# Two more regions for the rows: units five and six read while the loop drains

## The chip, the cores and the metric

The kernel runs on one core of a Trainium2 chip. The metric is the device time of one execution in microseconds (us). A profiled execution also has a span, which is the stretch from its first to its last instruction as the hardware profiler saw it; all positions below ("at 1138 us") are counted from the span's start.

## The reference

Two layers over x of 2 x 4096 tokens by D = 1024 channels, 8192 rows in all.

```python
# layer 1: gated linear recurrence, state S of 64 x 1024 for each sequence
shift = silu(causal_depthwise_conv(x, conv_w, conv_b))          # width 4
r, k  = split(shift @ in_proj_w.T)                               # 64 each
u     = sigmoid(x @ w0.T @ w1.T + b1) * x
sel, tau = softplus(mg[:64]), sigmoid(mg[64:])                   # mg = shift @ mem_gate_w.T + b
k     = k / norm(k) * sel ** tau;   g = -sel * tau
S     = exp(g) * S + k u;           o = r S / 8                  # step by step
y     = layernorm(x + o + shift * residual_weight)
# layer 2: every row chooses one of 64 tiles of 16 channels, by signs
xn    = layernorm(y) * gamma + beta
tile  = best of 64, from sign(xn) against the tiles' signatures
mn, mx = min and max, over ALL rows that chose the tile, of their 16 channels
delta = spline(tile, (xn[16 channels] - mn) / (mx - mn)) * output_scale[tile]
out   = layernorm(y + y + delta put into those 16 channels)
```

The smallest and largest value of a tile go over all rows, so the second half of layer 2 can only begin when layer 1 is done with its last row.

## The kernel before

The kernel consists of two programs in one launch, each written engine by engine with hand-placed semaphores. A barrier over all engines stands between them.

**The first program, the loop.** The rows are worked in 32 groups of 256 (`NG`, `T`), two chunks of 128 rows each. Group k passes through stages that are up to four steps apart, so a step works on several groups at once; SyncE (SP) issues the plain DMAs. For each group SP stores y (the rows before normalisation) twice: to `y_ring`, a small buffer in DRAM, and to `y_scratch`, which holds all rows. Later GpSimd (POOL) issues four indirect DMAs for the group, the gather (L1448 and L1451, `gsl` and `gbs`): for each row the 16 channels of its chosen tile from `y_ring`, and that tile's gamma and beta from a table. It then waits for them at L1465 and computes with them (`collect`, L1465 to L1473, whose last result is `xfs`). VectorE (DVE) takes the extremes over all rows in four parts (`extremes`, L1020 to L1033); the last part, rows of chunks 56 to 63, waits for the collect of the last group. After it comes the barrier. The choice of tile for a group comes from a matmul that TensorE (PE) ends with L474; its event is `e_key`, and e_key of the last group is the last read of the tiles `sg` and `yn`.

**The second program.** The rows come back from `y_scratch` in 16 units of 512 rows (2048 KB each). Units 0 to 14 go round eight places in SBUF (`slots`), unit 15 is still in `y_all`. A unit is read into its place, ScalarE (ACT) scales and shifts it there in four instructions (L1700), and ACT issues its store to `out` (L1707). Beside that PE and DVE work out the spline (`Z`, L1668 to L1823) in seven batches of chunks, POOL turns a batch's sums into coefficients (L1610 to L1619), and POOL puts the 16 corrected channels of each row into `out` by indirect DMAs, the scatters (L1629), one for each chunk of 128 rows, 64 in all; 28 of them come after the last batch's coefficients. A scatter of a unit waits until the unit's store has landed.

**The places.** A place is either a region that the loop's tiles have lain in, over which a unit may be read as soon as the loop has finished with it, or memory of the second program's own. `PRE` counts the former and `OWN` the latter. Before, they are five and three: units 0 and 1 are issued at L410 and L411 when the last group's projections are done, unit 2 at L437 and units 3 and 4 at L440 and L441 after the last state update. Units 5, 6 and 7 have places of their own and are issued at L1578, the first thing that SP does behind the barrier. Units 8 to 14 follow at the same line, each behind a wait for the store of the unit that had its place.

Of the kernel before, what the change touches and what calls it, by code (L numbers as in the profile page):

```python
# [7 lines left out]
F32 = mybir.dt.float32  # L8
BF16 = mybir.dt.bfloat16
F16 = mybir.dt.float16  # L10
# [4 lines left out]
P = 128  # L15
CH = 128
CPG = 2
T = CH * CPG
LEVELS = 7
# [28 lines left out]
def build(nc, x, w_rk, w_mg, w0, w1, conv_w, conv_b, gate_b1, mem_b, res_w, gamma, beta, bases, slopes, oscale, out):  # L48
    B, L, D = x.shape
# [3 lines left out]
    NB = D // P  # L53
    NG = B * L // T
# [5 lines left out]
    TPC = NT // NCL  # L60
    HALF = 512
    TC = 2 * DS * GRID
    PRE, OWN = 5, 3
    EXT_ENDS = (16, 40, 56, 64)
    SLOTS4 = PRE + OWN + 1
    assert TC == HALF
# [14 lines left out]
    with ExitStack() as whole:  # L81
        def sbw(name, shape, dt=F32):
            return whole.enter_context(nc.sbuf_tensor(name, shape, dt))
# [21 lines left out]
        zT_all = sbw("zT_all", [P, 2, NB, T])  # L105
# [13 lines left out]
        with ExitStack() as loop_only:  # L119
# [2 lines left out]
            w0_sb = loop_only.enter_context(nc.sbuf_tensor("w0_sb", [P, NB, R], F32))  # L122
            w1_sb = loop_only.enter_context(nc.sbuf_tensor("w1_sb", [P, D], F32))
        ohT = sbw("ohT", [P, NC, P], BF16)
        slots = [xT_all[:].rearrange("p i b t -> p (i b t)")[:, 0:4 * D].rearrange("p (n d) -> p n d", n=4), rows1[:],
                 rows2[:, 0:4 * D].rearrange("p (n d) -> p n d", n=4), th_all[:],
                 zT_all[:].rearrange("p i b t -> p (i b t)").rearrange("p (n d) -> p n d", n=4)]
        r_ld = [whole.enter_context(nc.semaphore(f"r_ld{i}")) for i in range(SLOTS4)]
        x1s = sbw("x1s", [P, NC, DS])
        xfs = sbw("xfs", [P, NC, DS])  # L130
# [1 line left out]
        with ExitStack() as ctx:  # L132
            def sb(name, shape, dt=F32):
                return ctx.enter_context(nc.sbuf_tensor(name, shape, dt))
# [7 lines left out]
            def ev(name, per_group=1):  # L142
                return Event(sem(name), per_group)
# [33 lines left out]
            xin = [xin_all[:, i, :, :] for i in range(2)]  # L177
            xT = [xT_all[:, i, :, :] for i in range(2)]
            zT = [zT_all[:, i, :, :] for i in range(2)]
            tS = [sb(f"tS{i}", [P, T]) for i in range(2)]  # L180

            rr = sb("rr", [P, CH])
            kk = sb("kk", [P, CH])
            ksq = sb("ksq", [P, CH])
            xs = sb("xs", [P, 2, CH])
            xa = sb("xa", [P, 2, CH])
            ge = sb("ge", [P, 2, CH])
            gl = sb("gl", [P, 2, CH])
            gw1 = sb("gw1", [P, 2, CH])
            grw = sb("grw", [P, 2, CH])  # L190
            sel = sb("sel", [P, CH])
            lsel = sb("lsel", [P, CH])
            tau = sb("tau", [P, CH])
            gn = sb("gn", [P, CH])
            tl = sb("tl", [P, CH])
            nl = sb("nl", [P, CH])
            kn = sb("kn", [P, CH])
            bb = sb("bb", [P, CH])
            rkp = sb("rkp", [P, CH])
            RX = sb("RX", [P, CPG, CH + 1])  # L200
            keT_sb = sb("keT_sb", [P, P])
            Wm = sb("Wm", [P, CPG, LEVELS, CH // 2])
            AT = sb("AT", [P, CPG, CH])
            th = [[th_all[:, CPG * i + c, :] for c in range(CPG)] for i in range(2)]
            S = [sb(f"S{i}", [P, HALF]) for i in range(2)]
            y = [y_all[:, i, :, :] for i in range(2)]
            yn = [sb(f"yn{i}", [P, D]) for i in range(CPG)]
            sg = sb("sg", [P, NB, T], F16)
            key_u = sb("key_u", [P, CPG], U32)
            key_n = sb("key_n", [P, CPG], U32)  # L210
            gix = [sb(f"gix{i}", [P, 2, CPG], U32) for i in range(2)]
# [7 lines left out]
            mm = sb("mm", [P, 2, NC])  # L219
            ext_n = sb("ext_n", [P, 2, NT])  # L220
            scratch = xin_all[:].rearrange("p i c d -> p (i c d)")
            sq = sb("sq", [P, CPG, D], BF16)
            ysum = sb("ysum", [P, CPG])
            nm = [sb(f"nm{i}", [P, CPG]) for i in range(2)]
            ssm = sb("ssm", [P, CPG])
# [58 lines left out]
            e_key, e_km = ev("e_key"), ev("e_km")  # L284
            e_cq, e_ch, e_go, e_cp = ev("e_cq", 2), ev("e_ch"), ev("e_go"), ev("e_cp", 6)

            def wait(eng, e, k, i=0):
                eng.wait_ge(e.sem, e.at(k, i))

            def done(eng, e, k):  # L290

                wait(eng, e, k, e.count - 1)
# [58 lines left out]
            y_u = y_dram.rearrange("(u n p) d -> u p n d", n=4, p=P)  # L351

            @block.sync
            def _(sp):
# [84 lines left out]
                done(sp, e_su[1], NG - 1)  # L439
                sp.dma_start(slots[3], y_u[3]).then_inc(r_ld[3], 16)  # L440
                sp.dma_start(slots[4], y_u[4]).then_inc(r_ld[4], 16)  # L441
                for b in range(2):
                    sp.wait_ge(d_yst[b], NG * 16)

# [1436 lines left out]
```

## Time and profile before

| | |
|---|---|
| time before, median of 3 runs | 1308.65 us (1307.91 to 1309.11) |
| the profiled execution, its own time | 1311.31 us |
| its span | 1309.2 us |
| busy: PE, DVE, ACT, POOL | 1158.9, 1061.5, 951.7, 833.4 us |
| barrier between the programs | at about 1138 us |

The loop takes seven eighths of the span. A row of a timeline gives the start and the duration in us, the engine, the line, the operation, what it writes and reads, how many like it were merged, and in brackets the idle time in front of it and what ended that. A queue's name ends in q (SPq, ACTq): its rows are the issue of a DMA, not its transfer. Names of tiles have their numbers left out, so `own` stands for all three of the second program's own places and `rows` for rows1 and rows2.

### The profile page before, as it was taken

What the parts mean: (1) busy time and instruction counts of PE and PEld (TensorE: products, weight loads), DVE (VectorE), ACT (ScalarE), POOL (GpSimd) and SP (SyncE); (2) the same over time, 40 slices, a digit from 0 to 9 for tenths busy, and PEclk for the clock granted to TensorE, in tenths of its full rate; (3) what the DMA queues carried; (4) which work ended last, traced back from release to release, by engine and by line L of the source; (5) the groups of instructions that cost most, each with busy time, mean ns of one, the idle gap of its engine ahead of it and who ended that gap; (6) DMA issues with size and microseconds to landing.
All of it is one profiled execution on the core that took longest, in us unless ns stands there. A gap on an engine that the chain in (4) does not pass through costs nothing. (4 is left out here: it accounts for less than half of the span.)

```text
span 1309.2 us, 31773 instructions
## 1 busy us (share of the span) xinstructions
PE 1158.9 (89%) x9346; PEld 735.1 (56%) x9346; DVE 1061.5 (81%) x2508; ACT 951.7 (73%) x1809; POOL 833.4 (64%) x1692
## 2 busy tenths in 40 slices
PE   5799999999999999999999999999999965588700
PEld 4556666666666666666666666666666632333100
DVE  4888889999999999999999999998988765586710
ACT  5657888888888888888888888888888743444760
POOL 3125666767676767676767676767676665335576
PEclk9989999999999999999999999999999977655555
DMA  4112222222222222222222222222222116689993
GB/s 141 34 37 102 103 103 104 102 102 102 102 102 102 102 103 106 106 106 106 106 106 106 106 106 106 106 106 106 106 105 102 71 65 234 230 316 352 419 409 125
DMA packets 64115, 175.05 MB, mean 134 GB/s; under 512 B 11580, under 2 KB 23108, under 8 KB 64071
## 3 DMA queue, kind: packets, MB, share of 16 engines
q1 hardware_dynamic: 49430, 138.85, 28.7%
q10 hardware_dynamic: 8496, 33.56, 6.6%
q0 software_dynamic: 6144, 2.11, 1.2%
q8 instruction: 22, 0.36, 0.1%
q14 instruction: 23, 0.18, 0.0%
HBM read 69.06 MB, written 101.20 MB: 130 GB/s over the span
## 5 line engine op out<-in xcount | busy, mean ns | idle before, releaser
L1052 DVE SCALAR_TENSOR_TENSOR acc<-xT_all,cw_sb,acc 128x256 f32<-128x256 f32 x768 | 354.3, 520 | 7.2 <-ACT acc L751 7.1
L777 ACT ACTIVATE sg<-TX,bet,gam 128x256 f16<-128x256 f32 x256 | 129.5, 556 | 42.2 <-PE TX L464 42.2
L484 PE MATMUL PR<-xT_all,w_sb 128*128 128x256 f32 x512 | 139.1, 396 | 2.9 <-ACT xT_all L715 2.9
L1384 POOL TENSOR_TENSOR AT<-AT,Wm 128x128 f32<-128x128 f32 x224 | 114.8, 512 | 41.7 <-DVE AT L1078 25.9
L496 PE MATMUL WK<-w_sb,tS 128*128 128x512 f32 x256 | 138.3, 622 | 0.0
L751 ACT ACTIVATE acc<-xT_all,cb_sb,cw_sb 128x256 f32<-128x256 f32 x256 | 132.5, 592 | 4.8 <-DVE xT_all L1038 2.8
L538 PE MATMUL OB<-th_all,AT 128*128 128x512 f32 x256 | 124.4, 609 | 11.7 <-POOL AT L1384 10.2
L566 PE MATMUL PR<-shT,w_mg_sb 128*64 128x128 f32 x2048 | 128.0, 278 | 6.5 <-ACT shT L760 6.5
L566 PE MATMUL PR<-shT,w_rk_sb 128*64 128x128 f32 x2048 | 125.9, 276 | 0.0
L566 PEld LDWEIGHTS PR<-shT,w_rk_sb 128*64 128x64 f32 x2048 | 110.5, 137 | 26.3 <-issue 26.3
L566 PEld LDWEIGHTS PR<-shT,w_mg_sb 128*64 128x64 f32 x2048 | 112.5, 138 | 18.9 <-issue 12.0
L1396 POOL TENSOR_TENSOR X<-bb 128x64 f32<-128x64 f32 x224 | 91.3, 413 | 48.4 <-DVE bb L1145 45.0
L484 PEld LDWEIGHTS PR<-xT_all,w_sb 128*128 128x128 f32 x512 | 90.0, 195 | 36.8 <-issue 25.1
L1060 DVE SCALAR_TENSOR_TENSOR zT_all<-shT,rw_sb,xT_all 128x256 f32<-128x256 f32 x256 | 106.8, 480 | 1.9 <-PE OB L543 1.5
L1066 DVE SCALAR_TENSOR_TENSOR th_all<-th_all,xin_all 128x1024 f32<-128x1024 f32 x64 | 78.3, 1223 | 33.3 <-ACT th_all L730 33.3
L715 ACT ACTIVATE xT_all<-TX 128x512 f32<-128x512 f32 x128 | 75.5, 590 | 38.9 <-PE TX L455 37.5
L455 PE MATMUL TX<-ident,xin_all 128*128 128x128 f32 x512 | 82.6, 285 | 12.7 <-DMA xin_all<-in_x 7.3
L705 ACT ACT_TABLE_LOAD x72 | 92.4, 1283 | 1.3
L1448 POOL DMA_INDIRECT gsl<-y_ring,gix x64 | 68.6, 1072 | 38.8 <-POOL st L1423 28.9
L464 PE MATMUL TX<-ident,yn 128*128 128x128 f32 x512 | 82.0, 284 | 10.8 <-DVE yn L1212 6.6
L1436 POOL TENSOR_TENSOR nm<-ysum,consts 128x1 f32<-128x1 f32 x64 | 22.3, 348 | 102.9 <-ACT y_all L741 102.9
L455 PEld LDWEIGHTS TX<-ident,xin_all 128*128 128x128 f32 x512 | 59.3, 144 | 48.1 <-issue 29.0
(230 smaller groups left out, 2665.1 us busy)
## 6 DMA issues: line engine op xcount, KB each, us to landing
xin_all<-in_x SPq DMA_DIRECT2D x32, 1024.0 KB
y_ring<-y_all SPq DMA_DIRECT2D x32, 1024.0 KB, 4.1
y_scratch<-y_all SPq DMA_DIRECT2D x32, 1024.0 KB, 6.1
own<-y_scratch SPq DMA_DIRECT2D x5, 2048.0 KB, 16.1
out<-own ACTq DMA_DIRECT2D x5, 2048.0 KB, 19.9
rows<-y_scratch SPq DMA_DIRECT2D x4, 2048.0 KB, 12.3
out<-rows ACTq DMA_DIRECT2D x4, 2048.0 KB, 13.6
RX<-RE SPq DMA_DIRECT2D x128, 32.2 KB
```

What stands on the lines that cost most here:

```text
L455: i = pe.transpose(TX[:, (blk % 2) * T + c * P:(blk % 2) * T + (c + 1) * P], xin[b][:, c, blk * P:(blk + 1) * P], ident[:])
L484: i = pe.matmul(PR[:, 0:T], w0_sb[:, blk, :], xT[b][:, blk, HIST:HIST + T], start=(blk == 0), stop=(blk == NB - 1))
L496: pe.matmul(WK[h][:], tS[b][:, chunk_cols(c)], w1_sb[:, half_cols(h)], start=True, stop=False)
L538: pe.matmul(OB[:, half_cols(h)], AT[:, c, :], th[b][c][:, half_cols(h)], start=True, stop=False)
L566: i = pe.matmul(PR[chunk_rows(c), (at + n) * CH:(at + n + 1) * CH], w[:, blk, n * M:(n + 1) * M], shT[:, blk, chunk_cols(c)], start=(opens ...
L705: nc.scalar.add_instruction(mybir.InstLoadActFuncSet(name=nc.get_next_instruction_name(), act_func_set_id=which))
L751: nc.scalar.activation(acc[:, blk, :], xT[b][:, blk, 0:T], ACT.Identity, scale=cw_sb[:, blk, 0:1], bias=cb_sb[:, blk:blk + 1]).then_inc(e_ ...
L777: nc.scalar.activation(sg[:, blk, :], TX[:, (blk % 2) * T:(blk % 2 + 1) * T], ACT.Sign, scale=gam[:, blk:blk + 1], bias=bet[:, blk:blk + 1 ...
L1052: v.scalar_tensor_tensor(acc[:, blk, :], xT[b][:, blk, i:i + T], cw_sb[:, blk, i:i + 1], acc[:, blk, :], ALU.mult, ALU.add).then_inc(e_con ...
L1060: v.scalar_tensor_tensor(zT[b][:, blk, :], shT[:, blk, :], rw_sb[:, blk:blk + 1], xT[b][:, blk, HIST:HIST + T], ALU.mult, ALU.add).then_in ...
L1384: q.tensor_tensor(late, late, Wm[:, :, l, :].rearrange("p c (n h) -> p c n h", h=h), ALU.add)\
L1396: q.tensor_tensor(x_late, b_late, ref, ALU.subtract)
```

## The change

The small tiles of the gates and the convolution's sums (tS to rkp, and Wm) are laid out together, and a region rows3 is laid over them; the normalised rows, their signs and their squares (yn, sg, sq) are laid out together, and a region rows4 is laid over those. Units 5 and 6 are read into these two. The number of places stays at eight.

```diff
-    PRE, OWN = 5, 3
+    PRE, OWN = 7, 1
...
+            tS = [lsb(f"tS{i}", [P, T]) for i in range(2)]
+            rr = lsb("rr", [P, CH])
...
+            rkp = lsb("rkp", [P, CH])
+            Wm = lsb("Wm", [P, CPG, LEVELS, CH // 2])
+        rows3 = sbw("rows3", [P, 7 * T + 14 * CH + LEVELS * CH])
...
+            yn = [lsb(f"yn{i}", [P, D]) for i in range(CPG)]
+            sg = lsb("sg", [P, NB, T], F16)
+            sq = lsb("sq", [P, CPG, D], BF16)
+        rows4 = sbw("rows4", [P, 4, D])
...
-                 zT_all[:].rearrange("p i b t -> p (i b t)").rearrange("p (n d) -> p n d", n=4)]
+                 zT_all[:].rearrange("p i b t -> p (i b t)").rearrange("p (n d) -> p n d", n=4),
+                 rows3[:, 0:4 * D].rearrange("p (n d) -> p n d", n=4), rows4[:]]
...
                 sp.dma_start(slots[4], y_u[4]).then_inc(r_ld[4], 16)
+                sp.dma_start(slots[5], y_u[5]).then_inc(r_ld[5], 16)
+                done(sp, e_key, NG - 1)
+                sp.dma_start(slots[6], y_u[6]).then_inc(r_ld[6], 16)
                 for b in range(2):
                     sp.wait_ge(d_yst[b], NG * 16)
```

The first place is SP's list at the end of the first program, from the last group's stores to the barrier, before the change; in brackets is what an instruction waits for, and rows is rows2.

```order
L363 DMA y_ring<-y_all 128x2x1024 [waits e_y]
L364 DMA y_scratch<-y_all 128x2x1024
L437 DMA rows<-y_scratch 128x4x1024 [waits e_dec,d_rx,e_keT,e_A]
L440 DMA th_all<-y_scratch 128x4x1024 [waits e_su,e_o]
L441 DMA zT_all<-y_scratch 128x4x1024
L132 UNCONDITIONAL_BRANCH [waits d_yst1,d_yst0]
L1575 UNCONDITIONAL_BRANCH [waits barrier_Pool_Activation_PE_DVE_SP_release]
```

The same place after the change; rows is rows2, then rows3 and rows4.

```order
L374 DMA y_ring<-y_all 128x2x1024 [waits e_y]
L375 DMA y_scratch<-y_all 128x2x1024
L448 DMA rows<-y_scratch 128x4x1024 [waits e_dec,d_rx,e_keT,e_A]
L451 DMA th_all<-y_scratch 128x4x1024 [waits e_su,e_o]
L452 DMA zT_all<-y_scratch 128x4x1024
L453 DMA rows<-y_scratch 128x4x1024
L455 DMA rows<-y_scratch 128x4x1024 [waits e_key]
L166 UNCONDITIONAL_BRANCH [waits d_yst1,d_yst0]
L1589 UNCONDITIONAL_BRANCH [waits barrier_Pool_Activation_PE_DVE_SP_release]
```

Unit 5 is now issued directly behind unit 4 and waits for nothing more; unit 6 follows behind a wait for e_key of the last group.

The second place is SP's list at the start of the second program, before the change; p_st is the store of the unit that had the place.

```order
L1578 DMA own<-y_scratch 128x4x1024 x3
L1578 DMA xT_all<-y_scratch 128x4x1024 [waits p_st0]
L1578 DMA rows<-y_scratch 128x4x1024 [waits p_st1]
L1578 DMA rows<-y_scratch 128x4x1024 [waits p_st2]
L1578 DMA th_all<-y_scratch 128x4x1024 [waits p_st3]
L1578 DMA zT_all<-y_scratch 128x4x1024 [waits p_st4]
L1578 DMA own<-y_scratch 128x4x1024 [waits p_st5]
```

The same after the change.

```order
L1592 DMA own<-y_scratch 128x4x1024
L1592 DMA xT_all<-y_scratch 128x4x1024 [waits p_st0]
L1592 DMA rows<-y_scratch 128x4x1024 [waits p_st1]
L1592 DMA rows<-y_scratch 128x4x1024 [waits p_st2]
L1592 DMA th_all<-y_scratch 128x4x1024 [waits p_st3]
L1592 DMA zT_all<-y_scratch 128x4x1024 [waits p_st4]
L1592 DMA rows<-y_scratch 128x4x1024 [waits p_st5]
```

Only unit 7 is left of the three reads behind the barrier; all later reads wait for the same stores.

The third place is POOL's list at the end of the first program after the change, the last group's gather and its collect; apart from line numbers it reads the same before it.

```order
L1462 DMA gsl<-y_ring,gix 128x16 [waits e_cp,e_ch,d_yst1]
L1465 DMA gbs<-gb_table,gix 128x32
L1462 DMA gsl<-y_ring,gix 128x16
L1465 DMA gbs<-gb_table,gix 128x32
L1479 COPY last_all<-gix 128x2 [waits e_keep,d_gat1]
L1480 TENSOR_TENSOR xc<-gsl,nm_all 128x32
```

Nothing moves here, nor on PE and DVE; on ACT only the places of units 5, 6, 13 and 14 have other names.

## Rows read from the trace of the kernel before

**Rows 1.** The page: the span, and its DMA share in 40 slices.

```profile
span 1309.2 us, 31773 instructions
...
DMA  4112222222222222222222222222222116689993
```

**Rows 2.** Timeline of POOL in the second program: a wait for sums, and the last scatters.

```profile
1228.18 0.23 POOL L1610 TENSOR_SCALAR mean_n<-sums 128x12 f32<-128x12 f32 x1 [11.68 <-DVE sums L1823]
...
1267.20 1.07 POOL L1629 DMA_INDIRECT out<-outs,gidx  x1 [0.86 <-DVE outs L1808]
...
1301.39 0.96 POOL L1629 DMA_INDIRECT out<-outs,gidx  x1 [0.30 <-issue]
```

**Rows 3.** Timeline of ACT in the second program: units 5 and 6.

```profile
1200.95 4.63 ACT L1700 ACTIVATE own<-own,coef 128x1024 f32<-128x1024 f32 x4 [0.46 <-ACT zT_all L1700]
...
1211.17 4.63 ACT L1700 ACTIVATE own<-own,coef 128x1024 f32<-128x1024 f32 x4 [5.59 <-POOL coef L1619]
```

**Rows 4.** Timeline of SP's queue from the last group's stores on.

```profile
1103.60 0.47 SPq L364 DMA_DIRECT2D y_scratch<-y_all  x1
1104.24 0.89 SPq L437 DMA_DIRECT2D rows<-y_scratch  x1
...
1106.54 1.37 SPq L441 DMA_DIRECT2D zT_all<-y_scratch  x1
1138.53 1.48 SPq L1578 DMA_DIRECT2D own<-y_scratch  x3
```

**Rows 5.** Stretches: length, busy time by engine, PE's clock, DMA share, GB/s.

```profile
1088.00:1090.00 2.00, 0.00 (x0) 0.00 (x0) 0.35 (x1) 0.47 (x2) 1.69 (x5) 1.00 0.91 313
...
1112.00:1114.00 2.00, 1.09 (x4) 0.71 (x4) 1.95 (x3) 0.29 (x1) 1.70 (x2) 0.50 1.03 420
...
1124.00:1126.00 2.00, 1.79 (x30) 1.63 (x28) 0.00 (x0) 1.92 (x2) 1.66 (x6) 0.50 1.00 399
1126.00:1128.00 2.00, 1.78 (x30) 1.62 (x28) 0.00 (x0) 1.55 (x3) 1.59 (x2) 0.50 0.17 28
...
1154.00:1156.00 2.00, 2.00 (x4) 0.32 (x4) 1.97 (x8) 2.00 (x2) 0.00 (x0) 0.50 0.89 354
```

**Rows 6.** DMA queues from 1103 to 1128 us: packets, MB, share.

```profile
q1 hardware_dynamic: 2128, 8.39, 88.7%
```

**Rows 7.** Timeline of the drain: gathers of groups 29, 30, 31, and the barrier.

```profile
1086.14 0.94 POOL L1451 DMA_INDIRECT gbs<-gb_table,gix  x1 [0.30 <-issue]
...
1091.62 0.18 POOL L1465 COPY last_all<-gix 128x2 uint32 x1 [0.86 <-DMA gbs<-gb_table,gix]
...
1116.38 1.77 POOL L1451 DMA_INDIRECT gbs<-gb_table,gix  x1 [0.30 <-issue]
...
1122.32 0.62 PE L474 MATMUL TX<-w_key,sg 128*128 128x8 f16 x16
...
1122.60 0.18 POOL L1465 COPY last_all<-gix 128x2 uint32<-128x2 uint32 x1 [4.44 <-DMA gbs<-gb_table,gix]
...
1124.80 1.01 POOL L1448 DMA_INDIRECT gsl<-y_ring,gix  x1
...
1128.61 0.94 POOL L1451 DMA_INDIRECT gbs<-gb_table,gix  x1 [0.31 <-issue]
...
1131.02 0.18 POOL L1465 COPY last_all<-gix 128x2 uint32<-128x2 uint32 x1 [1.47 <-DMA gbs<-gb_table,gix]
...
1132.60 0.17 DVE L1020 CAST idx_all<-last_all 128x8 f32<-128x8 uint32 x1 [8.68 <-POOL xfs L1473]
...
1138.56 0.29 DVE L1723 COPY ext<-ext 128x256 f32<-128x256 f32 x1 [0.53 <-PEq L132]
```

**Rows 8.** DMA issues from 1245 to 1266 us: scatters, count, us to landing.

```profile
out<-outs,gidx POOLq DMA_INDIRECT x12, 6.5
```

**Rows 9.** The same from 1286 to 1309 us.

```profile
out<-outs,gidx POOLq DMA_INDIRECT x13, 2.1
```

More of the change, by code:

```diff
@@ L124, in build, with lsb @@
         ohT = sbw("ohT", [P, NC, P], BF16)
+        with ExitStack() as loop_only:
+            def lsb(name, shape, dt=F32):
+                return loop_only.enter_context(nc.sbuf_tensor(name, shape, dt))
+            tS = [lsb(f"tS{i}", [P, T]) for i in range(2)]
+            rr = lsb("rr", [P, CH])
+            kk = lsb("kk", [P, CH])
+            ksq = lsb("ksq", [P, CH])
+            xs = lsb("xs", [P, 2, CH])
+            xa = lsb("xa", [P, 2, CH])
+            ge = lsb("ge", [P, 2, CH])
+            gl = lsb("gl", [P, 2, CH])
+            gw1 = lsb("gw1", [P, 2, CH])
+            grw = lsb("grw", [P, 2, CH])
+            sel = lsb("sel", [P, CH])
+            lsel = lsb("lsel", [P, CH])
+            tau = lsb("tau", [P, CH])
+            gn = lsb("gn", [P, CH])
+            tl = lsb("tl", [P, CH])
+            nl = lsb("nl", [P, CH])
+            kn = lsb("kn", [P, CH])
+            bb = lsb("bb", [P, CH])
+            rkp = lsb("rkp", [P, CH])
+            Wm = lsb("Wm", [P, CPG, LEVELS, CH // 2])
+        rows3 = sbw("rows3", [P, 7 * T + 14 * CH + LEVELS * CH])
+        with ExitStack() as loop_only:
+            def lsb(name, shape, dt=F32):
+                return loop_only.enter_context(nc.sbuf_tensor(name, shape, dt))
+            yn = [lsb(f"yn{i}", [P, D]) for i in range(CPG)]
+            sg = lsb("sg", [P, NB, T], F16)
+            sq = lsb("sq", [P, CPG, D], BF16)
+        rows4 = sbw("rows4", [P, 4, D])
         slots = [xT_all[:].rearrange("p i b t -> p (i b t)")[:, 0:4 * D].rearrange("p (n d) -> p n d", n=4), rows1[:],
                  rows2[:, 0:4 * D].rearrange("p (n d) -> p n d", n=4), th_all[:],
-                 zT_all[:].rearrange("p i b t -> p (i b t)").rearrange("p (n d) -> p n d", n=4)]
+                 zT_all[:].rearrange("p i b t -> p (i b t)").rearrange("p (n d) -> p n d", n=4),
+                 rows3[:, 0:4 * D].rearrange("p (n d) -> p n d", n=4), rows4[:]]
         r_ld = [whole.enter_context(nc.semaphore(f"r_ld{i}")) for i in range(SLOTS4)]
@@ L179, in build @@
             zT = [zT_all[:, i, :, :] for i in range(2)]
[L180 to L199, printed above, removed]
             RX = sb("RX", [P, CPG, CH + 1])
             keT_sb = sb("keT_sb", [P, P])
-            Wm = sb("Wm", [P, CPG, LEVELS, CH // 2])
             AT = sb("AT", [P, CPG, CH])
@@ L206, in build @@
             y = [y_all[:, i, :, :] for i in range(2)]
-            yn = [sb(f"yn{i}", [P, D]) for i in range(CPG)]
-            sg = sb("sg", [P, NB, T], F16)
             key_u = sb("key_u", [P, CPG], U32)
@@ L221, in build @@
             scratch = xin_all[:].rearrange("p i c d -> p (i c d)")
-            sq = sb("sq", [P, CPG, D], BF16)
             ysum = sb("ysum", [P, CPG])
```

## The prediction

> **What bounds the kernel now.** The change touches nothing before about 1107 us, so I read the page only for the span and the DMA share [rows 1]: the loop runs at a share of about two tenths, the end of it at six, the second program at eight to nine tenths. That invites the thought that DMA bounds the second program, and that reads taken out of it are time gained. So next I read who waits there. POOL is the engine that ends the span. Its last 28 scatters start from 1267.20 to 1301.39 us, 27 steps of 1.27 us, each with 0.30 us of idle time in front [rows 2]: they go at POOL's own pace and no store holds them up. What POOL waits for earlier are DVE's sums, as at 1228.18 us after 11.68 us [rows 2]. ACT, the only reader of the units, comes to unit 5 at 1200.95 us, straight from unit 4, and to unit 6 at 1211.17 us after a wait for POOL's coefficients [rows 3]. No wait of the second program is for a read of a unit.
>
> Then the drain of the loop, read backwards from the barrier. DVE's first instruction behind the barrier is at 1138.56 us. The last part of the extremes begins at 1132.60 us, after DVE has been idle for 8.68 us for POOL's xfs; that is the collect of group 31, the last group, which begins at 1131.02 us after 1.47 us of idle time for the gather's DMAs; their first is issued at 1124.80 us and their last at 1128.61 us [rows 7]. So the path to the barrier is gather, landing, collect, last extremes. A microsecond on the landing is one on the barrier, and all that stands behind it moves along.
>
> Last, what the DMA engines do meanwhile. SP issues y_scratch at 1103.60 us, unit 2 at 1104.24 and unit 4 at 1106.54 us, with unit 3 between them [rows 4]. They keep the engines full, at 420 GB/s in 1112 to 1114 us and 399 GB/s in 1124 to 1126 us; in 1126 to 1128 us it is 28 GB/s [rows 5]. The plain DMAs are done at about 1126 us. The gather of group 31 meets nearly idle engines; that of group 30 met full ones.
>
> **The change part by part.**
>
> *Unit 5.* Its issue, 2048 KB, now follows unit 4's, at about 1107.9 us (1106.54 + 1.37 [rows 4]). SP's queue moved 8.39 MB from 1103 us on [rows 6], at some 0.40 MB per us, so 2.10 MB take 5.2 us. Where the queue ran dry at about 1126 us, it now runs to about 1131.3 us.
>
> *Unit 6.* It waits for e_key of the last group, whose matmul ends at 1122.94 us (1122.32 + 0.62 [rows 7]). Queued behind that wait on SP are only two waits for y stores and the end of the program. SP is at the barrier some 15 us before it opens, so the wait costs nothing (it would cost only if e_key came later than 1138 us). The transfer stands behind unit 5's and runs to about 1136.5 us.
>
> *What they lie upon.* The four DMAs of group 31's gather are issued from 1124.80 to 1129.55 us, now with full engines throughout. What that does to the landing I read from the two gathers that met full engines. From the end of the last issue to the collect it took group 31 1.47 us (1129.55 to 1131.02). It took group 30 4.45 us (1118.15 to 1122.60) and group 29 4.54 us (1087.08 to 1091.62) [rows 7], with 313 GB/s in the stretch right after its last issue [rows 5]. The differences are 3.0 and 3.1 us. I take **+3.1 us**.
>
> The bounds. Below: nothing at all, if the gather got through as before. Above: group 30's last issue took 1.77 us instead of 0.94 [rows 7]. If full DMA engines do that, and to both table gathers of a group, it adds 1.7 us, 4.7 us in all. I don't take it: the last 28 scatters began while the engines were still full (the last of the page's nines stands for 1244 to 1276 us [rows 1]), and steps of 1.27 us leave no room for an issue of 1.77 us. DVE was busy during group 30's issues (1.95 of 2.00 us) and is idle during group 31's (0.00 in both stretches from 1124 us on [rows 5]). The Trainium skill, page "SBUF — State Buffer", section "SBUF: two separate sides", tells of a port that DVE and GpSimd share and lock, so that a DVE instruction can hold up GpSimd's writing of descriptors. By that rule the 1.77 us are DVE's doing and the addition is 0; by the row alone it could be 1.7 us. A third row of the same kind is the scatters': 6.5 us to landing under full engines and 2.1 us with idle ones [rows 8, 9], +4.4 us, though there two queues of plain DMAs ran beside them. It lies within the bounds.
>
> *Units 5 and 6 gone from behind the barrier.* Of three reads issued at 1138.53 us [rows 4] one is left, so the engines are full for 5 us there and not up to 1156 us (354 GB/s in 1154 to 1156 us [rows 5]). The first reader is ACT at 1200.95 us [rows 3], and even unit 7 comes after that. Gain: 0. It is hidden by ACT's 45 us of lead.
>
> *Places and tiles.* Units 13 and 14 wait for the same two stores as before, in rows3 and rows4 instead of own places. Instructions on PE, DVE and POOL are the same. The small tiles have other addresses; the trace gives no reason for a price, 0.
>
> *Sum.* 1311.31 us for the profiled execution + 3.1 = 1314.4 us. That execution lies 2.66 us above the median of the runs shown, so on the median 1308.65 + 3.1 = **1311.7 us**. That is 0.24% slower; a measurement of this kernel tells about 0.2% (2.6 us) from no change.
>
> **The rivals.**
>
> *The gather slips through (no change).* Each DMA engine may take turns between the queues, so that a gather waits one plain packet at a time. A plain packet is 8.39 MB / 2128 = 3.9 KB [rows 6], and one of the 16 engines moves it in about 0.16 us. With 8 of a gather's 128 rows to an engine and one turn for each row that is 1.3 us for one gather; with one turn for each gather, 0.2 us. Time: 1308.9 to 1310.0 us. The Trainium skill, page "DMA: Bandwidth & Descriptors", section "Queues, rings and completion order", states just this, that an engine alternates between its queue rows by packets. By the rule alone the sum would be about 1309 us. Against it stand groups 29 and 30, which lost 3.0 us and more under the same load.
>
> *Issues stretch too (slower).* As the upper bound: +4.7 us, 1313.4 us. It decides if the last gather issue takes 1.77 us with DVE idle.
>
> *The second program is bound by DMA after all (faster).* Place: the stretch from 1180 to 1280 us with full engines, and scatters that wait for stores. Two units are 4.2 MB, 10.5 us of the engines' time. If stores gated the scatters, taking these reads away early would bring up to 10.5 us, less 3.1: 1301.3 us. The share of the page speaks for it [rows 1]. Against it: the scatters' idle time is a constant 0.30 us [rows 2], and the two reads ran before the engines filled with stores, so the full stretch keeps all its work. It decides only if a scatter of units 9 to 14 waits for its store by over 3 us in the trace before, and none does.
>
> *The early reads help no one and hurt no one.* As the first rival with a price of nothing: 1308.65 us. I count it with the first.
>
> **How the numbers follow.** Delay of about 3.1 us on the landing: 0.57. Slips through or costs nothing: 0.28. Stretched issues: 0.08. Faster: 0.07. The prediction is the likeliest, 1311.7 us. The range takes in the bounds from nearly nothing (less the runs' own spread of about 0.6 us) to +4.7 us with that spread: 1308.2 to 1314.0 us; outside it are the faster case and the edges of the others, under 2 in 10. For the signs: the likeliest case lies only 0.5 us beyond the 0.2%, so of its 0.57 I give a fifth to "same". Slower 0.57 x 0.8 + 0.08 = 0.54; same 0.28 + 0.11 = 0.39; faster 0.07.
>
> **What the profile after would show.** Units 5 and 6 issued at about 1108 and 1123 us; full engines to about 1136 us with no dip; L1465's counterpart for the last group after an idle time of about 4.5 us and not 1.47; DVE's wait for xfs 11.8 us and not 8.68; the first instruction behind the barrier at about 1141.6 us; from there every row 3.1 us later and none nearer, the last scatter at about 1304.5 us, with 0.30 us of idle time in front. I would be wrong if the collect came at its old time although the engines are full, if the barrier came late for another reason, such as SP still waiting in it, or if the second program were shorter than before by some microseconds.

## The result

The changed kernel took 1312.14 us at the median of 9 runs (1309.02 to 1317.49), the kernel before 1308.51 us beside it (9 runs, 1306.21 to 1311.24): ratio 1.0034, 95% interval 1.0019 to 1.0050. It is slower, by about 4.4 us. Run again beside the experiments it was at 1.0025 (1.0013 to 1.0037), 3.3 us.

The profiled execution was the fastest of the nine, and on its face the trace says the opposite: its span is 2.3 us shorter than the one of before. The page, its first line and the DMA share:

```profile
span 1306.9 us, 31773 instructions
...
DMA  4112232222222222222222222222222117849993
```

One has to compare stretches, not spans. SP's timeline of the drain after the change (rows is rows2, then rows3 for unit 5 at L453 and rows4 for unit 6 at L455):

```profile
1097.81 0.37 SPq L374 DMA_DIRECT2D y_ring<-y_all  x1
...
1101.20 1.40 SPq L452 DMA_DIRECT2D zT_all<-y_scratch  x1
1102.63 4.74 SPq L453 DMA_DIRECT2D rows<-y_scratch  x1
1117.59 0.37 SPq L455 DMA_DIRECT2D rows<-y_scratch  x1
1136.27 0.37 SPq L1592 DMA_DIRECT2D own<-y_scratch  x1
```

The last group's store to y_ring starts at 1097.81 us. Before the change it started at 1103.19 us, 0.41 us ahead of L364 in [rows 4]:

```profile
1103.19 0.37 SPq L363 DMA_DIRECT2D y_ring<-y_all  x1
```

The loop up to there was 5.4 us shorter in this one execution, and everything below has to be read from that store on. POOL's and DVE's timeline, which answers to [rows 7]:

```profile
1119.39 1.00 POOL L1462 DMA_INDIRECT gsl<-y_ring,gix  x1 [0.20 <-issue]
...
1123.21 0.94 POOL L1465 DMA_INDIRECT gbs<-gb_table,gix  x1 [0.30 <-issue]
...
1128.76 0.18 POOL L1479 COPY last_all<-gix 128x2 uint32<-128x2 uint32 x1 [4.61 <-DMA gbs<-gb_table,gix]
...
1130.34 0.17 DVE L1034 CAST idx_all<-last_all 128x8 f32<-128x8 uint32 x1 [11.76 <-POOL xfs L1487]
...
1136.30 0.29 DVE L1737 COPY ext<-ext 128x256 f32<-128x256 f32 x1 [0.53 <-PEq L166]
```

The gather's issues are as before, 0.94 to 1.00 us each with 0.30 us between. Then POOL waits 4.61 us where it waited 1.47, and DVE 11.76 us where it waited 8.68. From the store to DVE's first instruction behind the barrier it is 38.49 us (1136.30 - 1097.81), and was 35.37 (1138.56 - 1103.19). The stretches of the changed kernel show why (columns as in [rows 5]):

```profile
1121.00:1123.00 2.00, 1.79 (x30) 1.64 (x28) 0.00 (x0) 1.02 (x1) 1.60 (x2) 0.50 1.04 414
1123.00:1125.00 2.00, 0.80 (x13) 0.64 (x12) 0.00 (x0) 1.02 (x1) 0.94 (x1) 0.50 1.04 399
...
1129.00:1131.00 2.00, 0.00 (x0) 0.00 (x0) 0.62 (x2) 0.00 (x0) 1.07 (x5) 0.50 0.98 389
1131.00:1133.00 2.00, 0.00 (x0) 0.00 (x0) 1.83 (x6) 0.00 (x0) 0.00 (x0) 0.50 0.15 61
```

The DMA engines are full through the whole gather and until about 1131.3 us, 33.5 us after the store, where before they were idle 23 us after it. Behind the barrier nothing has changed. ACT reaches unit 5 from unit 4 without a wait for the read, and the last scatter has the same 0.30 us in front of it as in [rows 2, 3]:

```profile
1198.69 4.64 ACT L1714 ACTIVATE rows<-rows,coef 128x1024 f32<-128x1024 f32 x4 [0.46 <-issue]
...
1299.14 0.95 POOL L1643 DMA_INDIRECT out<-outs,gidx  x1 [0.30 <-issue]
```

From the first instruction behind the barrier to the end of the span it is 170.6 us before (1309.2 - 1138.56) and 170.6 us after (1306.9 - 1136.30).

### The profile page after: what moved, and what is told of

It reads as the page before. It is cut to its first block and busy times, and to the rows that moved or that the text cites. A ratio compares the mean times of both kernels' runs of the same rounds, so it can differ in the third digit from the quotient of the medians.

```text
span 1306.9 us, 31773 instructions
## 1 busy us (share of the span) xinstructions
PE 1152.5 (88%) x9346; PEld 732.3 (56%) x9346; DVE 1060.8 (81%) x2508; ACT 953.0 (73%) x1809; POOL 834.6 (64%) x1692
## 5 line engine op out<-in xcount | busy, mean ns | idle before, releaser
L1226 DVE TENSOR_SCALAR yn<-y_all,nm,st 128x1024 f32<-128x1024 f32 x64 | 51.6, 809 | 41.7 <-POOL st L1437 41.7
```

## The experiments

All ratios are against the kernel before, from runs on the same chip. "The gather" is the last group's unless another is named, "idle engines" are the DMA engines with no plain DMA on them, and a read that is "held" waits until POOL is done with the collect of the last group (`e_cp`).

**The changed kernel again**, no edit.

> The changed kernel once more, for its time beside the others. In its first trace the last group's gather landed 4.61 us after its last issue, against 1.47 before, and DVE waited 11.76 us for it against 8.68; but its nine times spread from 1309.0 to 1317.5 us and their median is 3.6 us above that of before. Landing theory (the whole loss is the gather's landing under full DMA engines): +3.1 us, ratio 1.0024, the waits of 4.6 and 11.8 us again in the trace. Rival (something in the loop is dearer too, such as the new addresses of the small tiles): +4 to +5 us, ratio 1.0035.

Ratio 1.0025 (1.0013 to 1.0037). In its trace the wait at the last collect is 5.20 us:

```profile
1134.10 0.18 POOL L1479 COPY last_all<-gix 128x2 uint32<-128x2 uint32 x1 [5.20 <-DMA gbs<-gb_table,gix]
```

Its interval holds the 3.1 us of the landing theory, and the upper part of it does not exclude 4.

**The layout alone.** Regions as in the change, reads as before it.

```diff
-                sp.dma_start(slots[5], y_u[5]).then_inc(r_ld[5], 16)
-                done(sp, e_key, NG - 1)
-                sp.dma_start(slots[6], y_u[6]).then_inc(r_ld[6], 16)
...
-                for u in range(PRE, NS):
+                for u in range(PRE - 2, NS):
```

> Only the layout of the change: rows3 and rows4 lie over the small tiles and serve units 5 and 6, but both units are read where they were before, directly behind the barrier. Landing theory: as before, 0 us (ratio 1.000), the last gather lands 1.5 us after its last issue and DVE waits 8.7 us for xfs. Rival of the addresses: +1 us or more with these two waits as before, the time being lost in the 1080 us of the loop.

Ratio 1.0005 (0.9996 to 1.0014). The addresses are not where the loss comes from; 0.5 us, or up to 1.8 us, is not excluded. The wait at the last collect was 2.80 us and not 1.5, although the engines were idle as in the kernel before (share 0.17 in 1126 to 1128 us in both):

```profile
1132.36 0.18 POOL L1476 COPY last_all<-gix 128x2 uint32<-128x2 uint32 x1 [2.80 <-DMA gbs<-gb_table,gix]
```

**Both reads early, but behind the gather.**

```diff
-                sp.dma_start(slots[5], y_u[5]).then_inc(r_ld[5], 16)
-                done(sp, e_key, NG - 1)
+                done(sp, e_cp, NG - 1)
+                sp.dma_start(slots[5], y_u[5]).then_inc(r_ld[5], 16)
                 sp.dma_start(slots[6], y_u[6]).then_inc(r_ld[6], 16)
```

> The changed kernel with the reads of units 5 and 6 still in the first program, but held until POOL is done with the collect of the last group (at about 1132.5 us of the trace of before), six microseconds ahead of the barrier. Landing theory: 0 us against before (1.000), and 3 us less than the changed kernel: wait of 1.5 us for the gather, engines idle from 1126 us until the reads begin. Rival (what costs is reads in flight at the barrier, or SP late in it): +3 us as in the changed kernel, with the loss behind 1132 us.

Ratio 1.0003 (0.9990 to 1.0015): the loss is gone with both reads still in flight at the barrier (393 GB/s in 1136 to 1138 us). POOL and SP in its timeline:

```profile
1131.12 0.18 POOL L1479 COPY last_all<-gix 128x2 uint32<-128x2 uint32 x1 [2.17 <-DMA gbs<-gb_table,gix]
...
1132.69 0.37 SPq L454 DMA_DIRECT2D rows<-y_scratch  x1
...
1133.10 0.51 SPq L455 DMA_DIRECT2D rows<-y_scratch  x1
```

So what costs is that the reads overlap the gather, neither that they are in flight at the barrier nor that they are issued ahead of it.

**One read early, the other behind the barrier.** First unit 5, then unit 6.

```diff
# unit 5 alone
-                done(sp, e_key, NG - 1)
-                sp.dma_start(slots[6], y_u[6]).then_inc(r_ld[6], 16)
...
-                for u in range(PRE, NS):
+                for u in range(PRE - 1, NS):
# unit 6 alone
-                sp.dma_start(slots[5], y_u[5]).then_inc(r_ld[5], 16)
...
-                for u in range(PRE, NS):
+                for u in (5, 7):
```

> Only unit 5 is read early, directly behind unit 4; unit 6 is read behind the barrier, into rows4. The queue of plain DMAs then runs dry at about 1131.3 us of the trace of before and not at 1136.5 us, while the last gather is issued up to 1129.55 us. Landing theory: the gather gets through soon after 1131.3 us, so about half of the loss, +1 to +2 us (ratio 1.0008 to 1.0015), the wait at its collect between 2.5 and 4 us. Rival (any read in flight costs the full 3 us): ratio 1.0024. Rival (it is unit 6 and SP's wait for the key that cost): 1.000.

> Only unit 6 is read early, behind SP's wait for the last key; unit 5 is read behind the barrier, into rows3. The plain DMAs are 2048 KB more as in the kernel with unit 5 alone, and end at the same 1131.3 us, since the queue is still full at 1123 us. Landing theory: the same +1 to +2 us as there. Rival (SP's wait or place in the queue matters): this one alone costs 3 us, and the one with unit 5 nothing.

Both 1.0016 (1.0004 to 1.0028, and 1.0005 to 1.0026), 2.1 us. The waits at the last collect, of unit 5 alone:

```profile
1130.54 0.18 POOL L1477 COPY last_all<-gix 128x2 uint32<-128x2 uint32 x1 [3.62 <-DMA gbs<-gb_table,gix]
```

and of unit 6 alone:

```profile
1129.40 0.18 POOL L1478 COPY last_all<-gix 128x2 uint32<-128x2 uint32 x1 [3.46 <-DMA gbs<-gb_table,gix]
```

Both units give the same, so it is not which unit it is, nor SP's wait for the key. That half of the data costs half is what the waits say, 3.5 us between 2.3 with idle engines (the mean of the table below) and 4.9 with both reads early. The timed runs alone don't say it: 1.0024, the rival by which any read costs the full 3 us, lies in both intervals. The ratios are a little above the forecast band, the waits within it.

**All five reads behind the gather**, units 2 to 6, so that the gather of group 30 meets idle engines too.

```diff
-                sp.dma_start(slots[2], y_u[2]).then_inc(r_ld[2], 16)
                 done(sp, e_o[1], NG - 1)
                 done(sp, e_su[1], NG - 1)
+                done(sp, e_cp, NG - 1)
+                sp.dma_start(slots[2], y_u[2]).then_inc(r_ld[2], 16)
...
-                done(sp, e_key, NG - 1)
```

> As e4, with the reads of units 2, 3 and 4 held until the same point too, so that the gathers of both group 30 and group 31 meet DMA engines that carry only the y stores. Landing theory: group 30's gather lands 1.5 us after its last issue and not 4.45. Then the next gather is not held up by it but by the choice of tiles, which DVE ends at 1123.9 us, some 0.8 us before POOL now begins it: -0.7 us against before (ratio 0.9995), and nothing lost in the second program, since ACT reads unit 2 at 1173 us and 10.5 MB take 26 us from 1133 us, to 1159 us. Group 30's table issues stay at 1.77 us if DVE makes them long, and fall to 0.95 us if the full DMA engines did. Rival (the second program is short of DMA time): slower than before by 2 us or more.

Ratio 1.0036 (1.0020 to 1.0053): slower, where I expected a small gain. Its timeline, and the stretch around the longest issue (columns as in [rows 5]):

```profile
1112.60 0.94 POOL L1462 DMA_INDIRECT gsl<-y_ring,gix  x1 [0.31 <-issue]
1112.67 0.42 DVE L1040 TENSOR_REDUCE mm<-xfs 128x16 f32<-128x256 f32 x1
...
1113.58 1.23 DVE L1044 TENSOR_TENSOR xin_all<-xin_all,mm 128x1024 f32<-128x1024 f32 x1
1113.85 1.78 POOL L1465 DMA_INDIRECT gbs<-gb_table,gix  x1 [0.30 <-issue]
...
1117.09 0.27 POOL L1479 COPY last_all<-gix 128x2 uint32<-128x2 uint32 x1 [1.47 <-DMA gbs<-gb_table,gix]
...
1122.20 1.00 POOL L1462 DMA_INDIRECT gsl<-y_ring,gix  x1 [2.91 <-DVE gix L1246]
...
1132.58 3.20 SPq L454 DMA_DIRECT2D rows<-y_scratch  x1
...
1135.83 4.87 SPq L455 DMA_DIRECT2D rows<-y_scratch  x1
1136.14 0.29 DVE L1047 TENSOR_TENSOR ext<-ext,ext_n 128x128 f32<-128x128 f32 x1
1141.21 0.16 POOL L1607 MEMSET mh<- 128x64 f32 x1 [10.24 <-POOLq L166]
1141.22 4.43 SPq L1592 DMA_DIRECT2D own<-y_scratch  x1
1141.26 0.29 DVE L1737 COPY ext<-ext 128x256 f32<-128x256 f32 x1 [4.82 <-PEq L166]
...
1113.00:1115.00 2.00, 0.49 (x3) 0.09 (x1) 1.90 (x4) 1.02 (x2) 1.70 (x2) 0.50 0.12 11
```

Group 30's gather did land early, after 1.47 us, but nothing came of it: POOL then waited 2.91 us for the choice of tiles and began the last gather 21.53 us after the y_ring store, against 21.61 us (1124.80 - 1103.19) before. My 0.7 us had counted the time between DVE's end of the choice and POOL's issue as a delay by group 30. It is 0.8 us here too (1121.39 to 1122.20), though POOL stands waiting, so there was nothing to win. And SP, whose fifth issue took 4.87 us, was done at 1140.70 us, when DVE had been ready since 1136.43; it held the barrier 4.3 us.

Two other things can be read here. The issue of a table gather took 1.78 us with the DMA engines all but idle (share 0.12), so it is not full DMA engines that make it long. It is not a busy DVE as such either: right before it an issue took 0.94 us while DVE ran instructions of 0.42 us, and the long one lies beside one of 1.23 us. And the last scatters end as far behind the barrier as ever (1311.9 - 1141.26 = 170.6 us), so the late reads did not lengthen the second program.

**Three and four reads behind the gather**, to separate SP's full queue from lateness. (That the queue is full is read from the length of the issues; no row shows the queue itself.) Three: the kernel before with units 2 to 4 held as above. Four: the changed kernel with units 2 to 5 held, units 6 and 7 behind the barrier.

> The kernel before with the reads of units 2, 3 and 4 held until POOL's collect of the last group, and units 5 to 7 behind the barrier as before. With all five reads held, the gathers of groups 30 and 31 both met idle engines, but SP's issue of unit 6 took 4.87 us because its queue was full, SP came to the barrier 4 us late, and the kernel was 0.36% slower than before. Theory of SP's full queue: three issues do not fill it, SP is at the barrier before DVE, and the time is that of before or up to 1 us less (ratio 0.9992 to 1.000). Rival (reads that come later starve the second program of DMA time): slower than before by 2 us or more, with SP on time in the barrier.

> Four reads held until POOL's collect of the last group, units 2 to 5, and units 6 and 7 behind the barrier: between the kernel with three held, which took the time of before, and that with five held, which was 0.36% slower. Theory of SP's full queue: in the kernel with five held the fourth issue took 3.20 us and ended 0.6 us ahead of DVE's last extremes, and only the fifth ran over; so with four SP is just in time, DVE's idle time at the barrier is 0.53 us and not 4.82, and the time is that of before (ratio 1.000 to 1.001). Rival (each read that comes later than the loop costs the second program a share): ratio 1.002, between the two.

Ratios 1.0004 (0.9992 to 1.0017) and 1.0003 (0.9991 to 1.0014). With four held:

```profile
1135.17 3.41 SPq L454 DMA_DIRECT2D rows<-y_scratch  x1
1138.72 0.29 DVE L1046 TENSOR_TENSOR ext<-ext,ext_n 128x128 f32<-128x128 f32 x1
1139.52 4.44 SPq L1591 DMA_DIRECT2D rows<-y_scratch  x1
1139.55 0.29 DVE L1736 COPY ext<-ext 128x256 f32<-128x256 f32 x1 [0.53 <-PEq L166]
...
1174.44 1.13 POOL L1642 DMA_INDIRECT out<-outs,gidx  x1 [5.47 <-DMA out<-xT_all]
```

SP is done at 1138.58 us, 0.4 us before DVE, and the barrier's idle time is back at 0.53 us. The loss of the kernel with five held was SP's full queue, and it begins with the fifth read. The late reads are not without effect, though: a scatter of unit 0 now waits 5.47 us for its store (5.25 with three held). It costs nothing because POOL's next wait, for DVE's sums, is shorter by as much (7.58 and 7.80 us, 12.32 in the kernel before).

**The opposite of the change**: the kernel before with units 5 to 7 read 27 us later.

```diff
+                sp.wait_ge(p_st[0], 16)
                 for u in range(PRE, NS):
```

> The kernel before with the reads of units 5, 6 and 7 not at the barrier but behind the landing of the first store, at about 1165 us, 27 us later: the opposite of the change. Theory (no wait of the second program is for these reads before 1200 us, so reading them earlier has nothing to win): as before within 0.5 us (ratio 1.000), the three reads done at about 1182 us beside two more stores. Rival (the second program is bound by DMA from 1180 us on, so 6.3 MB more there cost up to 15 us): slower by 5 us or more, with scatters that wait for stores.

Ratio 1.0025 (1.0014 to 1.0036): 3.3 us, which neither theory gave. Its second program is 173.3 us long (1312.3 - 1139.00) instead of 170.6, with no wait of ACT for a read of a unit. POOL's timeline:

```profile
1201.15 0.96 POOL L1630 DMA_INDIRECT out<-outs,gidx  x1 [4.61 <-DMA out<-rows]
...
1261.54 0.96 POOL L1630 DMA_INDIRECT out<-outs,gidx  x1 [2.86 <-DMA out<-xT_all]
```

and ACT's, where the issue of a store takes 4.96 us (0.38 in the kernel before):

```profile
1242.90 4.96 ACTq L1708 DMA_DIRECT2D out<-rows  x1
1247.91 4.63 ACT L1701 ACTIVATE th_all<-th_all,coef 128x1024 f32<-128x1024 f32 x4 [5.04 <-issue]
```

The three reads push the stores back until scatters wait for them. The wait at 1201 us is swallowed by POOL's next wait for DVE, 0.57 us where it was 4.85. The one at 1261 us, between two of the scatters that go 0.30 us apart in the kernel before, is not: it is 2.56 us longer, nearly all of the 2.7 us. ACT's long issues cost nothing more, since no later scatter waits. Two stretches of the kernel before show where its engines have room:

```profile
1155.00:1160.00 5.00, 3.89 (x12) 1.13 (x12) 3.41 (x12) 4.48 (x5) 0.00 (x0) 0.50 0.27 107
...
1220.00:1230.00 10.00, 9.74 (x18) 1.75 (x17) 8.21 (x29) 5.54 (x5) 1.58 (x6) 0.50 1.02 420
```

Its reads of units 5 to 7 end at about 1156 us, ahead of a pause. The change took work out from in front of this pause, where it had cost nothing; reads that come behind it push on the stores.

No kernel here beats the one before: four of them reach its time.

The drains of all traces side by side, in us. The second column is the start of the last y_ring store, the third the wait at the last collect, the fourth runs from the store to DVE behind the barrier, the fifth from there to the end of the span.

| kernel | store at | wait | to the barrier | behind it |
|---|---|---|---|---|
| before | 1103.19 | 1.47 | 35.37 | 170.6 |
| layout alone | 1103.16 | 2.80 | 36.73 | 170.6 |
| both behind the gather | 1102.57 | 2.17 | 36.08 | 170.6 |
| three held | 1100.00 | 2.26 | 36.22 | 170.5 |
| four held | 1103.26 | 2.46 | 36.29 | 170.5 |
| units 5 to 7 late | 1102.37 | 2.66 | 36.63 | 173.3 |
| unit 5 alone early | 1100.55 | 3.62 | 37.53 | 170.6 |
| unit 6 alone early | 1099.45 | 3.46 | 37.49 | 170.7 |
| changed kernel | 1097.81 | 4.61 | 38.49 | 170.6 |
| changed kernel again | 1102.44 | 5.20 | 39.20 | 170.7 |
| five held | 1100.67 | 2.47 | 40.59 | 170.6 |

## Why the prediction was right

**Where it would be lost.** The step was that the two reads lie upon the last gather and that a microsecond on its landing is one on the barrier. The traces show it, and the experiments confirm it: the reads moved behind the gather take the loss away, and with half of the data the added wait is about half.

**The size, +3.1 us.** Measured ratios make it 4.4 and 3.3 us, the two traces 3.1 and 3.8 us against the one trace of before. But this term was taken against a landing of 1.47 us, and that was the shortest of the seven with idle engines; their mean is 2.3 us and that of the two full ones 4.9, a difference of 2.6 us. In the column to the barrier, without the kernel with five held, it is 38.85 - 36.22 = 2.6 us as well. So the mechanism accounts for 2.6 us, and the timed runs show 0.7 to 1.8 us more at their centres, with intervals that reach down to 1.7 us. The layout's 0.05% would fit in that gap, but its interval holds zero: what the rest is stays open. That the forecast of 1311.7 us came within 0.5 us of the measured median is therefore in part luck: the term was taken 0.5 us too large, and the unexplained rest, or the spread of the runs, made up for it.

**Unit 5 and unit 6.** The queue was forecast to run dry at about 1136.5 us, 33.3 us after the store; it was 33.5. One thing I had not counted with did no harm: the issue of unit 5 took 4.74 us, against 1.40 for unit 4. SP had to wait for e_key until 1117.59 us anyway.

**The upper bound, stretched issues.** Not in force: 0.94 and 0.95 us for the table gathers under full engines, and 1.78 us under idle ones beside a DVE instruction of 1.23 us. The rule of the Trainium skill, page "SBUF — State Buffer", section "SBUF: two separate sides", that a DVE instruction can hold up GpSimd's writing of descriptors, fits both; that it is this port no run here shows.

**The gather slips through.** The trace decides against it: 4.6 and 5.2 us instead of at most 2.8. With one plain packet of 3.9 KB, some 0.16 us, at a time the extra wait came out at 0.2 to 1.3 us; it was 2.6. So one record of the profile at a time is not how long the gather waits. The Trainium skill, page "DMA: Bandwidth & Descriptors", section "Queues, rings and completion order", is not refuted by that. It says that an engine drains a whole packet, typically 9 to 17 descriptors, before it turns to the next queue, and I had taken one record of the profile for such a packet. If a record is one descriptor, a turn is 1.4 to 2.7 us, an estimate from the page's 9 to 17 and the 0.16 us. No run here shows what a turn holds.

**Nothing gained behind the barrier.** Right, to 0.1 us. The reason I gave was incomplete. That no wait is for a read is true, but the late reads cost 2.7 us without any such wait, by way of the stores. The rival "bound by DMA after all" is half true: three reads brought in at 1165 us cost time, while two taken from before 1160 us return nothing.

## What to carry to other kernels

A read that is moved up to where "the DMA engines are idle" has to be checked against the small transfers on the path there: four gathers of 128 rows, on which all engines wait at a barrier, landed 2.6 us later under two plain reads of 2 MB. Let the big reads wait for the last small one's landing and not only for the buffer to be free. Here that only avoids the loss and wins nothing. So ask first what the place they come from was short of; here it had slack.

A loss of 3 us in a kernel whose loop alone varies by 5 us is not to be read from two spans: measure from the last common event to the next.

## What the runs showed of the hardware

SP's issue of a plain DMA of 2048 KB took 0.37 to 1.64 us for the first three in a row. The fourth, begun with idle engines, took 3.20 and 3.41 us and the fifth 4.87; behind two y stores and three reads the next took 4.74, 5.71 and 5.74 us in three traces. SP did nothing else in that time: with five reads held it came to the barrier 4.3 us late.

With idle engines the last gather landed between 1.47 and 2.80 us after its last issue, in seven traces of the same instructions; why it varies no run shows. And the start of the last y_ring store lay anywhere from 1097.81 to 1103.26 us over the eleven traces.
